# The down product of the shared network, issued two inner chunks behind its gate and up products

## The reference, cut to what matters

```python
def _swiglu_mlp(x, wg, wu, wd):
    return jax.nn.silu(x @ wg) * (x @ wu) @ wd
...
return y + _swiglu_mlp(identity, sw_gate, sw_up, sw_down)   # inner width 352 * 2 = 704
...
x = x + gb * _L0_ffn_ref(h, ...)
```

## Time and profile before

| | |
|---|---|
| median of 3 runs (lowest to highest) | 3312.66 us (3307.47 to 3314.26) |
| the profiled execution, its own time | 3308.82 us |
| its span, first to last instruction | 3307.1 us |
| busy share of the span | PE 88%, DVE 76%, PEld 49%, ACT 48%, POOL 27% |
| mean granted clock of PE | 0.944 of full speed |
| the shared network | from about 2853 us to the end of the span |

### The profile page before, as it was taken

How to read it: one execution, slowest core, us unless ns; L and a number is a source line. 1 busy time by engine, 2 the same in 40 slices (tenths; PEclk the granted TensorE clock), 3 DMA queues, 4 the chain that set the end, 5 groups by cost and what they waited for, 6 DMA issues and landing times. The chain is left out here.

```text
span 3307.1 us, 61435 instructions
## 1 busy us (share of the span) xinstructions
PE 2912.5 (88%) x22508; PEld 1616.0 (49%) x22508; DVE 2518.0 (76%) x4678; ACT 1588.5 (48%) x2160; POOL 884.5 (27%) x1100
## 2 busy tenths in 40 slices
PE   6885699999999999999999996873999999788888
PEld 3553133333333333333333325763888888677776
DVE  5885989888898888898888914664777777566665
ACT  2542166666676666666666782221444444111111
POOL 5773010111110111101111112664222222333332
PEclk8997699999999999999999997775999999899999
DMA  4776111122111212111221005664444455332332
GB/s 132 204 209 186 49 35 47 48 54 53 43 44 49 54 48 57 38 46 48 55 52 43 20 8 160 212 198 167 155 155 155 156 159 156 105 94 85 96 97 73
DMA packets 388533, 317.93 MB, mean 96 GB/s; under 512 B 112720, under 2 KB 374844, under 8 KB 388288
## 3 DMA queue, kind: packets, MB, share of 16 engines
q1 hardware_dynamic: 370752, 277.67, 29.4%
q0 software_dynamic: 12288, 33.57, 3.0%
q10 hardware_dynamic: 5248, 3.41, 0.4%
HBM read 196.89 MB, written 116.93 MB: 95 GB/s over the span
## 5 line engine op out<-in xcount | busy, mean ns | idle before, releaser
L903 ACT ACTIVATE probs<-ps_s 128x1024 f32<-128x1024 f32 (+3 forms) x1280 | 1077.9, 896 | 599.2 <-PE ps_s L1071 598.6
L926 DVE TENSOR_REDUCE piece_rest<-ps_m 128x1 f32<-128x512 f32 (+2 forms) x1260 | 748.8, 646 | 91.8 <-PE ps_m L1046 42.0
L1071 PE MATMUL ps_s<-q_st,k_st 50*128 50x512 bf16 (+7 forms) x5120 | 594.4, 346 | 19.0 <-ACT probs L903 15.2
L1086 PE MATMUL ps_o<-probs,vs 128*32 128x512 f32 (+3 forms) x5120 | 600.8, 541 | 4.3 <-POOL probs L883 1.2
L883 POOL TENSOR_SCALAR_AFFINE_SELECT probs<-probs 128x256 f32<-128x256 f32 x512 | 204.9, 406 | 1481.2 <-ACT probs L903 1476.0
L926 DVE TENSOR_REDUCE piece_late<-ps_m 128x1 f32<-128x512 f32 x900 | 548.8, 666 | 33.0 <-PE ps_m L1038 17.9
L1038 PE MATMUL ps_m<-k_st,q_st 48*128 48x512 bf16 (+3 forms) x2400 | 407.5, 353 | 65.8 <-DVE piece_rest L926 48.1
L1038 PEld LDWEIGHTS ps_m<-k_st,q_st 48*128 48x128 bf16 x2400 | 106.9, 93 | 651.8 <-DVE piece_rest L926 339.0
L1071 PEld LDWEIGHTS ps_s<-q_st,k_st 50*128 50x128 bf16 (+1 forms) x5120 | 224.1, 95 | 250.8 <-ACT probs L903 91.0
L1803 ACT ACTIVATE act_g<-ps_g 128x512 f32<-128x512 f32 x117 | 69.9, 597 | 279.5 <-PE ps_u L1895 279.5
L1840 DVE TENSOR_TENSOR hid_f<-act_g,ps_u 128x512 f32<-128x512 f32 x117 | 80.5, 688 | 126.8 <-ACT act_g L1803 126.8
(11 more groups left out here) (228 smaller groups left out, 5103.2 us busy)
## 6 DMA issues: line engine op xcount, KB each, us to landing
k_st<-qk_parts SPq DMA_DIRECT2D x768, 32.0 KB, 1.8
qk_parts<-parts SPq DMA_DIRECT2D x124, 192.0 KB, 2.9
q_st<-qk_parts SPq DMA_DIRECT2D x720, 32.0 KB, 1.8
x_r<-expert_rows SPq DMA_DIRECT2D x39, 512.0 KB, 4.6
expert_made<-made SPq DMA_DIRECT2D x39, 512.0 KB, 2.9
x_in<-in_L_attn_x_dram SPq DMA_DIRECT2D x32, 512.0 KB, 4.7
vs<-v_ones SPq DMA_DIRECT2D x64, 256.0 KB, 3.7
v_ones<-v_out SPq DMA_DIRECT2D x60, 256.0 KB, 4.7
```

What stands on the lines that cost most here:

```text
L903: act.activation(probs[:, u % PSLOTS, 2 * pair:2 * pair + 2, j * P:ST], ps_s[:, pair, :, j * P:ST], ACT.Exp, scale=SCALE).then_inc(exp_don ...
L926: v.tensor_reduce(dst, ps_m[:, bank, 0:n * w].rearrange("p (n w) -> p n w", n=n), AX.X, ALU.max) \
L1071: last = pe.matmul(ps_s[:, pair, z, j * P:ST], k_st[rows, slot, half, pair, kc * P:(kc + 1) * P], q_st[rows, slot, half, pair, qt * ST + j ...
L1086: last = pe.matmul(ps_o[h * VW:(h + 1) * VW, j * P:ST], vs[:, slot, kc, h * VW:(h + 1) * VW], probs[:, u % PSLOTS, h, j * P:ST], start=(kc ...
```

## The change

A constant `LAG` = 2 is added, and three places of the loops are written in its terms. On PE `down` follows `up` two chunks behind and no longer one. On DVE `finish(u - 1)`, with the copies `weight_now` and `gb_now` behind it, moves from behind `hidden(u, 0)` to behind `hidden(u, 2)`, and `low_rows(u + 1)` from behind `hidden(u, 2)` to behind `hidden(u, 4)`. `mix_experts` stays behind `hidden(u, 3)`. The programs of ACT, POOL and SP have the same instructions in the same order as before. No tile or buffer changes size, and no instruction is added or removed.

```diff
+    LAG = 2
...
-                        if i == 0 and not (first and slot == 0):
+                        if i == LAG and not (first and slot == 0):
                             finish(u - 1, 1 - slot)
-                        if i == 0 and slot == 0:
+                        if i == LAG and slot == 0:
                             v.wait_ge(gated_done, it * 2 + 1)
...
-                        if i == 2 and not (last and slot):
+                        if i == LAG + 2 and not (last and slot):
                             low_rows(u + 1, 1 - slot)
...
                         up(u, i, slot)
-                        if i > 0:
-                            down(u, i - 1, slot)
+                        if i >= LAG:
+                            down(u, i - LAG, slot)
                         elif not (first and slot == 0):
-                            down(u - 1, NC - 1, 1 - slot)
+                            down(u - 1, NC + i - LAG, 1 - slot)
...
-            down(NST - 1, NC - 1, 1)
+            for i in range(NC - LAG, NC):
+                down(NST - 1, i, 1)
```

## The result

The changed kernel takes 3442.15 us (median of 4 runs, 3437.94 to 3444.35) beside 3312.72 us for the kernel before: the ratio is 1.0392, with a 95% interval of 1.0374 to 1.0410. The forecast of a slower kernel was right in its sign and in the path that it named; the time lies 24 us above the predicted 3418 and 4 us above the range. The profiled execution took 3444.35 us, with a span of 3442.6.

The account below looks back on a forecast made before the run. The late load of the next supertile, in a ring through `finish` and `y_out`, was taken to bound the kernel. Profiled 3308.8 + 104 (14 x 7.4) - 2 (head and tail) + 7 (clock) = 3418 us; range 3400 to 3438.

Parts of the forecast that it names:

- the ring: `finish`, `y_out`, store, `h` load, `h_high`: the chain starts at SiLU 2, not SiLU 0, 8.32 us later.
- second wait: PE before `up` of the next chunk 0, for `h_low` moved behind `hidden(u, 4)`: 4.3 us, 1.5 to 4.3 after slow clock.
- first wait: PE before `up` of chunk 5, for `hid_f` of chunk 3: 7.0 us per supertile.
- the term of the clock: Half clock on `up` of the next chunk 0: 0.5 us per period, 7 us in all, bounds 0 and 23.
- the two short ones: PE's waits of 1.45 and 1.57 us before `down` in the kernel before, with no slow-clock row following.
- the upper bound of 23: Slow clock at `up` of the next chunk 0 in all 14 supertiles, 1.65 us lost each.
- rival 3: PE's clock falls at both waits in each supertile: 3434 us; chance 12%.
- paid before and after alike: Slow `h` loads, 1.6 us longer in four of 14 periods, were claimed to cost the same in both kernels.
- rival 4: The load changes speed by its new place: all slow 3434 us, all fast 3412; 8% for the slow side.
- the forecast's 3.5: From the end of `h_low` to SiLU 0: 3.0 us, and 0.5 for the clock.
- between 0 and -4: Head and tail: PE's waits of 4 us outside the fourteen periods may go; taken as -2 us.

Follow-up runs that it names:

- early load: Kernel before, with the load of `h` on its own semaphore and issued one supertile earlier, `down` one chunk behind: 3262.79 us, ratio 0.9853.
- the version with the early load and the lag: Changed kernel, with the load of `h` issued one supertile earlier on its own semaphore: 3300.28 us, ratio 0.9968.
- filler products: Changed kernel plus unused PE products, 28 ahead of `up` of chunk 5 and 14 behind `down` of chunk 3, in supertiles 1 to 14: 3427.61 us, ratio 1.0352.

## Why the prediction was right and wrong

**Right: what bounded the kernel.** PE's 46.2 us for `hid_low` were read as a consequence of the late load. The early load took them to 9.9 us without touching `down`.

**Right: the ring.** `finish` moved by two chunks and took `y_out`, SP's queue, `h_high` and the SiLU of chunk 3 with it; moved alone it costs all of the 129 us. The later `down` gives 40 us back, and the later `h_low` takes 41.

**Right: `low_rows`.** A second wait for `h_low` before chunk 0, all 14 times; taken back, 41 us return. Its length was predicted as 1.5 to 4.3 us behind a slow clock, and it is 2.2. The first wait was predicted as 7.0 us; the two on the timeline looked at were 7.78 and 8.76.

**Wrong: the term of the clock.** The step said "I take 0.5 per period, 7 us, nearer to none, since the shortened wait is near the two short ones". The second wait is indeed short, but the slow clock followed it in all fourteen supertiles, and it cost some 1.5 us each time: from the end of `h_low` to SiLU 0 it is 4.64 us in the mean, against 3.12 in the nine supertiles at full clock of the version with the gathers held back. That is 21 us, near the upper bound of 23, where 7 were taken. The step that failed is the inference from three lengths: 2.2 us is nearer to 1.45 and 1.57 than to 2.93, but it acted like the latter. The long wait before it is not needed for that, since in the version with the early load and the lag a wait of 1.84 to 2.10 us alone does the same in twelve of fourteen supertiles. The length does not decide by itself, though: in the two others waits of 1.99 and 2.10 us brought no slow clock, nor did 3.06 us behind the filler products. Of the 21 us the filler products returned 19. Of the Trainium skill, "TensorE: Matmul & The Clock Gate", section "HAM oscillation", the rule that a wait in every round brings the slow clock in every round was rival 3, given 12%; the clock rows of the changed kernel agree with it, in all fourteen.

**Wrong, by less: the load.** It was taken at 6.35 us as in the supertile looked at, with the slow ones "paid before and after alike". After the change all fourteen take longer, 6.91 to 7.93 us and 7.35 in the mean, against 6.8 before: 14 x 0.6 = 8 us. That is half of rival 4. Without the gathers the load takes 6.2 us, so they explain it; why more fall into it in the changed kernel is open. SP, POOL and the gathers have the same order in both.

**How the miss of 24 us adds up.** By the table, end of `h_low` to SiLU 0 is 1.14 us above the forecast's 3.5, 14 x 1.14 = 16 us. SiLU 2 to `h_high` is 15.35, where the forecast stood for 14.41 and the 0.45 by which the mean supertile of before exceeds the one looked at, 7 us. `h_high` to `h_low` is 0.13 shorter, 2 us less. That is 21 us. The sum also set out from the profiled execution, 3.9 us below the median of the kernel before, and added none of it. The "between 0 and -4" outside the fourteen periods, taken as -2, came out as -1: 135.5 - 5.0 - 131.6. The small rest is the spread between executions, so it is partly luck that the two large terms alone, 16 + 8, come to 24.

**Wrong: the range.** It left out the case that rivals 3 and 4 meet, as if they were alternatives. Nothing in the sum ties them together; the first happened almost in full and the second by half.

## What to carry to other kernels

Before a product is moved further behind its producer, ask what else was hung on the same place of the loop: here the epilogue of the last supertile released the buffers for the next load, and two chunks later for it was two chunks later for everything. A wait that a profile puts down to a slow engine can be a late DMA two engines upstream, so follow it back before curing it: one load issued a supertile earlier, with its own semaphore, gave 1.5%, and only then was the lag of two chunks, with the rest moved as little as it allows, worth another 0.5%. Costs that may each happen in every round must be added in a range, not set beside each other.

## What the runs showed of the hardware

PE's clock fell to half after waits of 1.87 to 2.44 us for `h_low` (changed kernel, all 14), of 1.84 to 2.10 (early load, lag 2; twelve supertiles of 27.3 to 27.6 us, but not in two of 25.9 and 26.0), and of 1.83 to 2.04 (gathers held back, five supertiles). Waits of 1.32 to 1.72 us there, and of 1.45 and 1.57 in the kernel before, did not bring it, and neither did one of 3.06 behind the filler products. So a short wait that comes back in every supertile can cost some 1.5 us each time, and its length alone does not say whether it will.

Some DVE instructions that start while POOL runs `y_out` end only after it: a CAST of 128x512 from 0.43 to 2.18 us, the 128x1024 subtract `h_low` from 1.22 to 3.30, but `hid_f`, which reads one operand from PSUM, keeps its 0.68. The Trainium skill, "GPSIMD Engine Reference", section "Specifications", says that POOL shares its SBUF interfaces with DVE, with contention for DVE instructions in a two-port mode or with two SBUF inputs; for `h_low`, with two inputs in SBUF, and `hid_f`, with one, these rows agree; in which mode the CAST runs no row shows. It goes the other way too: where `h_low` started 0.22 us before `y_out`, it kept its 1.22 and `y_out` took 3.25. Moving `finish` from behind `hidden(1)` to behind `hidden(2)` moved that meeting from a `hid_high` with slack to the `h_low` without, and set `finish` and `h_low` in a row. Together this cost 15 us; no run separates the two.
